# Unchosen spans of the picked sums: overwritten on VectorE instead of by a TensorE product, and a seventh picked slot

## The reference

```python
edge_index = jnp.stack([src, dst])
h = jnp.maximum(_layernorm(x, axis=-1), 0.0)
x = x + _L0_gnn_ref(h, edge_index, edge_attr_32, ...)     # relu([h[dst], h[src], attr] @ W1 + b1) @ W2 + b2, segment_sum
h = jnp.maximum(_layernorm(x, axis=-1), 0.0)
x = x + _L1_gnn_ref(h, edge_weight1, src, dst)            # softmax(edge weight) per dst times h[src], segment_sum, elu
h = jnp.maximum(_layernorm(x, axis=-1), 0.0)
x = x + _L2_gnn_ref(h, theta_w, theta_b, phi_w, phi_b, src, dst)  # (h[dst] - h[src]) @ theta + phi(h[src]), segment_max
h = jnp.maximum(_layernorm(x, axis=-1), 0.0)
x = x + _L3_gnn_ref(h, edge_index, edge_attr_16, ...)     # three-layer MLP on [h[src], h[dst], attr], segment mean
```

## Time and profile before

| | |
|---|---|
| median of 3 runs | 7793.15 us (7792.11 to 7808.14) |
| the profiled execution | 7796.36 us, of which the span of instructions is 7794.6 us |
| granted TensorE clock, mean | 0.941 |
| PE (matmul) busy | 6659.6 us, 85% |
| DVE busy | 5210.7 us, 67% |
| POOL busy | 5823.6 us, 75% |
| ACT busy | 2085.6 us, 27% |

### The profile page before, as it was taken

The page is one execution under the profiler, slowest core; times in us unless marked ns, Lnnn a source line. Parts: engine busy times, 40 slices in busy tenths (PEclk is TensorE's granted clock), DMA queues, the critical chain, the costliest instruction groups (busy, mean ns, idle before and its releaser), DMA issues.

```text
span 7794.6 us, 87563 instructions
## 1 busy us (share of the span) xinstructions
PE 6659.6 (85%) x29454; PEld 5473.0 (70%) x29454; DVE 5210.7 (67%) x6271; ACT 2085.6 (27%) x5004; POOL 5823.6 (75%) x6117
## 2 busy tenths in 40 slices
PE   0799999999669999999479999999139999999992
PEld 0688888888557777777367777777127777777771
DVE  6577777777667777777767777777545666666663
ACT  5133333333212222222300000000014444444441
POOL 7777777777777777777767777777777777777776
PEclk9999999999879999999689999999569999999995
DMA  8354544444323333333223333333124444444441
GB/s 321 84 113 112 113 111 113 112 112 113 84 62 83 82 82 88 82 82 82 59 63 74 74 74 77 75 74 74 44 59 98 100 98 98 98 98 99 98 99 42
DMA packets 1063994, 722.05 MB, mean 93 GB/s; under 512 B 583026, under 2 KB 970916, under 8 KB 1063428
## 3 DMA queue, kind: packets, MB, share of 16 engines
q1 hardware_dynamic: 850448, 510.81, 23.7%
q0 software_dynamic: 197008, 163.26, 13.7%
q10 hardware_dynamic: 16100, 42.39, 1.4%
HBM read 478.38 MB, written 237.49 MB: 92 GB/s over the span
## 4 chain that ended last, share of the span: by engine, by line
POOL 48%; issue 16%; PE 6%; DVE 3%; DMA 1%; ACT 0%; POOLq 0%; DVEq 0%
POOL G L683 42%; POOL R L702 5%; PE pOdd L905 4%; PE pRows L905 1%; POOL first_rows L644 1%; DVE onehot L1288 1%; DVE S L1337 1%; PE pRows L1002 0%; PE pOdd L897 0%; DVE G L1300 0%; ACT G L828 0%; DMA G<-table,e_dst 0%; DMA G<-table,idx 0%; DVE pT L1322 0%; DMA prefix<-O 0%
## 5 line engine op out<-in xcount | busy, mean ns | idle before, releaser
L683 POOL DMA_INDIRECT G<-table,idx x2923 | 2758.3, 944 | 891.0 <-issue 878.2
L683 POOL DMA_INDIRECT G<-table,e_dst x2497 | 2362.8, 946 | 790.7 <-issue 753.7
L1223 DVE TENSOR_TENSOR_SCAN K<-mask_f,K,pT 48x512 f32<-48x512 bf16 x782 | 1005.4, 1286 | 1242.5 <-PE pT L970 1117.0
L1002 PEld LDWEIGHTS pRows<-w,S 128*128 128x128 f32 x6256 | 1573.9, 324 | 304.4 <-issue 179.2
L905 PE MATMUL pOdd<-h_high,onehot 128*128 128x480 f32 (+1 forms) x3880 | 1519.5, 392 | 0.0
L905 PE MATMUL pOdd<-h_low,onehot 128*128 128x480 f32 (+1 forms) x3880 | 1489.6, 384 | 0.0
L1002 PE MATMUL pRows<-w,S 128*128 128x48 f32 x6256 | 1445.3, 374 | 2.1 <-ACT O L838 0.5
L905 PE MATMUL pRows<-h_high,onehot 128*128 128x480 f32 (+1 forms) x2430 | 952.6, 392 | 85.1 <-DVE h_low L1076 85.1
L905 PE MATMUL pRows<-h_low,onehot 128*128 128x480 f32 (+1 forms) x2430 | 920.4, 379 | 0.0
L1288 DVE TENSOR_TENSOR onehot<-mask_f,pEven 128x2560 fp32r<-128x2560 f32 (+1 forms) x390 | 892.1, 2288 | 19.4 <-DMA mask_f<-pick_row 19.4
L905 PEld LDWEIGHTS pOdd<-h_high,onehot 128*128 128x128 f32 x3880 | 749.8, 193 | 128.5 <-issue 3.9
(11 more groups left out here) (203 smaller groups left out, 8666.6 us busy)
## 6 DMA issues: line engine op xcount, KB each, us to landing
mask_f<-same_row SPq DMA_DIRECT2D x392, 256.0 KB, 3.3
prefix<-O SPq DMA_DIRECT2D x194, 512.0 KB, 3.6
G<-first_rows SPq DMA_DIRECT2D x784, 96.0 KB
prefix<-O SPq DMA_DIRECT2D x390, 192.0 KB
G<-table,idx POOLq DMA_INDIRECT x2923
G<-table,e_dst POOLq DMA_INDIRECT x2497
first_rows<-zeros ACTq DMA_DIRECT2D x14, 2688.0 KB, 15.5
K<-in_ea_dram SPq DMA_DIRECT2D x588, 64.0 KB
```

Of the source, the lines that this page charges most:

```text
L683: pool.indirect_dma_start(rows[:, slot, j, 0:widths[l]], None, table[l], bass.IndirectOffsetOnAxis(ap=at[:, n, j:j + 1], axis=0))\
L1002: last = pe.matmul(o, s[:, :, j], (w2_0 if l == 0 else w3_3)[:, :], start=True, stop=True)
L1223: dve.tensor_tensor_scan(K[r, c.slot, :], mask_of(c, r), pT[c.slot % 2][r, :], K[r, (c.slot - 1) % RING, CHUNK - 1:CHUNK], ALU.mult, ALU.add)\
```

## The change

The hiding product and `minus_big` go. The accumulation now starts with the first group's product. Ahead of each reduction VectorE runs one `scalar_tensor_tensor` in place on the accumulator, sums = unchosen * -3e38 + sums, over all picks of the duo, and waits for its completion (`link`). The same operation is placed in `place_edges` for layers 0 and 3. Slot 4 joins `PICK_SLOTS`, so seven of eight chunks pick in layers 1 and 2; `PICK_EXTRA` goes. In layers 0 and 3 the picked columns stay the same.

```diff
@@ -45,8 +45,7 @@
 QUAD = 32
 QUADS = P // QUAD
 PICK_SPAN = 10
-PICK_SLOTS = (1, 2, 3, 5, 6, 7)
-PICK_EXTRA = RING + 4
+PICK_SLOTS = (1, 2, 3, 4, 5, 6, 7)
 PICK_COLUMN = TJ - 1
 PICK_RING = 4
 EDGE_PICK_CYCLE = {0: 3, 3: 6}
...
@@ -59,7 +58,7 @@
 
 def stream_picks(chunks):
 
-    return [n for n in range(chunks) if n % RING in PICK_SLOTS or n % (2 * RING) == PICK_EXTRA]
+    return [n for n in range(chunks) if n % RING in PICK_SLOTS]
 
 
 def edge_picks(l, chunks):
...
@@ -892,25 +890,14 @@
                                              start=True, stop=True)
                         last.then_inc(hq_made, 1)
 
-            def hide_unchosen(out, i):
-
-                pe.matmul(out[:, 0:SPAN * D], minus_big[:, :],
-                          unchosen[:, i, :].rearrange("p (s o) -> p s o", o=1).to_broadcast([P, SPAN, D]),
-                          start=True, stop=False)
-
             def add_group(out, rows_of, g):
 
                 first, stop = g * SPAN, min((g + 1) * SPAN, B)
                 for part in (h_high, h_low):
                     last = pe.matmul(out[:, 0:(stop - first) * D], rows_of[:, g, :],
                                      part[:, first:stop, :].rearrange("p b d -> p (b d)"),
-                                     start=False, stop=g == PICK_GROUPS - 1 and part is h_low)
+                                     start=g == 0 and part is h_high, stop=g == PICK_GROUPS - 1 and part is h_low)
                 return last
-
-            def hide_unchosen_of(d):
-
-                for k, i in enumerate(picks_of(d)):
-                    hide_unchosen(pick_sum[d % 2][:, k, :], i)
 
             def add_rows(d, g):
 
...
@@ -935,7 +920,6 @@
                     pe.wait_ge(split_made, SPLIT_BEFORE[l] + 1)
                 for d in range(first, DUOS):
                     pe.wait_ge(picks_marked[l], d + 1 - FIRST_DUO[l])
-                    hide_unchosen_of(d)
                     for g in range(PICK_GROUPS):
                         last = add_rows(d, g)
                     last.then_inc(picks_summed[l], 1)
...
@@ -1014,7 +997,6 @@
                         if k == 0:
                             pe.wait_ge(edges_marked, EDGE_PICKS_BEFORE[l] + i + 1)
                             pe.wait_ge(split_made, SPLIT_BEFORE[l] + (1 if l == 0 else NQ))
-                            hide_unchosen(out, FIRST_PICK[l] + i)
                         for g in range(PICK_GROUPS * k // steps, PICK_GROUPS * (k + 1) // steps):
                             last = add_group(out, edge_onehot[i % len(edge_sum[l])], g)
                         if k == steps - 1:
...
@@ -1230,11 +1211,14 @@
                     if i is None:
                         return
                     dve.wait_ge(edges_summed, EDGE_PICKS_BEFORE[l] + i + 1)
-                    place_edges(i, c.slot, PICK_COLUMN)
-
-                def place_edges(i, slot, j, l=l):
+                    place_edges(i, FIRST_PICK[l] + i, c.slot, PICK_COLUMN)
+
+                def place_edges(i, flags, slot, j, l=l):
 
                     out = edge_sum[l][i % len(edge_sum[l])]
+                    sums = out[:, 0:SPAN * D].rearrange("p (b d) -> p b d", d=D)
+                    link(dve.scalar_tensor_tensor(sums, unchosen[:, flags, :].rearrange("p (b o) -> p b o", o=1)
+                                                  .to_broadcast([P, SPAN, D]), -BIG, sums, ALU.mult, ALU.add))
                     dve.tensor_reduce(G[:, slot, j, 0:D],
                                       out[:, 0:SPAN * D].rearrange("p (b d) -> p d b", d=D), AX, ALU.max)
 
...
@@ -1290,6 +1274,13 @@
                                       span_id.rearrange("p (k g o) -> p k g o", k=1, o=1)
                                       .to_broadcast([P, k, PICK_GROUPS, P]), ALU.is_equal).then_inc(picks_marked[l], 1)
 
+                def hide_unchosen(sums, i, k):
+
+                    sums = sums.rearrange("p k (b d) -> p k b d", d=D)
+                    flags = unchosen[:, i:i + k, :].rearrange("p k (b o) -> p k b o", o=1)
+                    link(dve.scalar_tensor_tensor(sums, flags.to_broadcast([P, k, SPAN, D]), -BIG, sums,
+                                                  ALU.mult, ALU.add))
+
                 def place_picks(d, l=l):
 
                     if d >= DUOS:
...
@@ -1297,6 +1288,7 @@
                     dve.wait_ge(picks_summed[l], d + 1 - FIRST_DUO[l])
                     picks = picks_of(d)
                     k, slot = len(picks), PICKS[picks[0]] % RING
+                    hide_unchosen(pick_sum[d % 2][:, 0:k, 0:SPAN * D], picks[0], k)
                     last = dve.tensor_reduce(G4[:, slot:slot + k, PICK_COLUMN, 0:D],
                                              pick_sum[d % 2][:, 0:k, 0:SPAN * D]
                                              .rearrange("p k (b d) -> p k d b", d=D), AX, ALU.max)
```

More of the change, by code:

```diff
@@ L189, in build @@
         ident = sb("ident", [P, P])
-        minus_big = sb("minus_big", [P, P], bf16)
         w1_0 = sb("w1_0", [P, HID])
@@ L863, in _ @@
         def _(pe):
-            pe.wait_ge(ident_done, 2)
+            pe.wait_ge(ident_done, 1)
             pe.wait_ge(G_zeroed, 1)
@@ L928, in sum_picks @@
                         for d in range(2):
-                            if g == 0:
-                                hide_unchosen_of(d)
                             last = add_rows(d, g)
@@ L954, in _ @@
                         out = edge_sum[0][i % 2]
-                        hide_unchosen(out, NP + i)
                         for g in range(PICK_GROUPS):
@@ L1147, in _ @@
             dve.wait_ge(ident_done, 1)
-            dve.tensor_scalar(minus_big[:, :], ident[:, :], -BIG, None, ALU.mult).then_inc(ident_done, 1)
             link(dve.tensor_tensor(seed[:, 0:1], ident[:, 49:50], ident[:, 82:83], ALU.add))
@@ L1368, in _ @@
                             n, j = EARLY[i - 2]
-                            place_edges(i, n % RING, j)
+                            place_edges(i, NP + i - 2, n % RING, j)
                         if i < len(EARLY):
```

## The result

| | before | after |
|---|---|---|
| median of the runs, us | 7792.63 | 8042.57 |
| its range, us | 7791.38 to 7808.14 | 8039.82 to 8046.96 |
| span of the profiled execution, us | 7794.6 | 8044.3 |
| mean granted clock of TensorE | 0.941 | 0.922 |

The change makes the kernel slower: the ratio is 1.0317, interval 1.0299 to 1.0334. The direction and the mechanism in layers 1 and 2 were forecast; the size and a loss in layer 3 were not, and 8042.6 lies above the range.

What follows compares the result with a forecast made beforehand. The prediction took GpSimd's gathers as the bound before, the TensorE - VectorE loop after: 7796.4 + 44 (loop and edges) + 73 (clock falls) = 7913 us for the profiled execution, so 7910 for the median; range 7835 to 8000.

Steps and rivals of the forecast that it cites:

- What bounds the kernel, and that the bound moves: Layers 1 and 2: GpSimd's gathers set the pace before; afterwards the TensorE - VectorE loop, 32.4 us a turn against 31.2.
- Part 3: VectorE's new operation in layers 1 and 2 stands inside the loop: 1.16 us for 960 elements, 1.20 us with its completion.
- far bound (0.6, 2.2): Limits for the new operation's time: 0.6 us if elements overlapped, 2.2 us if the accumulator were passed once each way.
- The loop without the clock: Layers 1 and 2 with TensorE's clock staying up: turns of 32.4 us, +44 us in total, 7840 us.
- The 0.12 us added to s1: Added per turn in layers 1 and 2, for a 128x128 float32 weight load now first after TensorE's wait.
- Part 4: TensorE's clock in layers 1 and 2: about 2.2 us idle every turn can bring falls costing 1.55 us each; +73 us.
- I take half the turns: Layers 1 and 2: clock falls assumed in half the turns, giving +73 us.
- the case "every turn": Layers 1 and 2: a clock fall in every turn, 94 x 1.55 = 146 us, time near 7983 us.
- Rival (a): Layers 1 and 2: the loop bounds but TensorE's clock stays up, 7837 us; chance 0.20.
- Layers 0 and 3 "come out at nothing": No cost in layers 0 and 3: VectorE's added 0.7 us in three or six chunks lies under its waits for TensorE.
- The bound named there, 99 us: Most that layers 0 and 3 would cost if VectorE's waits gave no cover: 142 x 0.7 = 99 us.
- Parts 1 and 2: Layers 1 and 2: 50 fewer gathers, worth 62.4 us if GpSimd stays the bound; TensorE's work 29.9 us under GpSimd's 31.2.

Runs made afterwards that it cites:

- the filler kernel: Changed kernel plus five TensorE products that nobody reads after each one-pick sum in layers 1 and 2: 7912.68 us, ratio 1.0133 to the kernel before.
- The one-product filler: Changed kernel plus one unread TensorE product, instead of five, after each one-pick sum in layers 1 and 2: 7997.08 us, ratio 1.0248.
- the last experiment: Kernel before the change with slot 4 always picked and layers 1 and 2's scans behind the one-hot, no VectorE operation: 7759.32 us, ratio 0.9935.

## Why the prediction was right in kind and wrong in size

**What bounds the kernel, and that the bound moves: right.** GpSimd's waits for VectorE's scan are there (145.8 us in layer 1; the forecast of some 60 was for the loop without falls, and the filler kernel, which has none, shows 75.6), and s1 starts on the one-hot.

**Part 3, the operation: right.** 1.163 us for 960 elements, 1.20 with the step to the reduction; forecast 1.16 and 1.20. The neighbouring rows of the same operation and the same memory gave it, and neither far bound (0.6, 2.2) had anything in it.

**The loop without the clock: right.** A turn of 32.44 us against 32.4; +25.1 and +25.8 us in the layers, by the filler kernel, against +21 and +23. The last 7 us are the allowance of 2 us a layer for the edges and 0.03 to 0.04 us a turn. The 0.12 us added to s1 had no row behind it; s1 without a fall takes 8.67 us, s2 and s3 8.57, so about that much is there. That the weight load is the reason, no run shows.

**Part 4, the clock: the mechanism right, the term mis-sized.** The idle was forecast at about 2.2 us and is 2.16; a fall at 1.55 us and is 1.53. What failed is "I take half the turns". Falls came in 43 of 48 turns in each layer, 131.5 us instead of 73. The rows before gave 2.08 (never) and 2.24 to 2.44 (five of six), and I read a threshold out of them, with 2.2 "between". The one-product filler shows that there is no sharp edge: 1.94 us in every turn, less than the 2.08 that brought no fall in the kernel before, did so in half the turns. That waits of this size were rare there, and return in every turn now, is the likely reason that their rate did not carry over; this is argued, no run tests it. The prediction had the case "every turn" worked out at 146 us and near 7983. Rival (a) falls: 86 falls stand behind 2.16 us of idle. The Trainium skill allows idle gaps of that length ("TensorE: Matmul & The Clock Gate", Why this matters for your kernels); this trace disagrees with it, and the measurement decides.

**Layers 0 and 3 "come out at nothing": wrong, and it put the time out of the range.** Layer 3 cost 60.7 us. The step that failed is "0.7 us more on VectorE in three or six chunks lies under its waits for TensorE". It set a total of waits against a total of added work. VectorE does wait in most chunks, but in the one chunk of six where the place, the one-hot and the scan meet, it is the other way round: TensorE, which has no time to spare in this layer, waits for the scan, 62 times and 40.2 us in all. It also left out that a fall of the clock can follow so short a wait. The bound named there, 99 us "that cover gone", would have held it, but the range left it out: with 7983 for falls in every turn and 60 us more, the forecast's own numbers reach 8043. The falls carry the loss: 46 of them at 1.6 us are 74 us, more than the 60.7 measured over the layer; where the rest is won back was not followed up. Why 46 of 62 equal waits bring a fall and 16 do not stays open. For layer 0 "nothing" was right. From 500 to 2050 us TensorE waits for the scan there once, for 0.5 us, and the 5.6 us by which layer 1 starts later are no sign of the operation: layer 1 starts at 2219.9 us with it in the run with the scan behind the one-hot, as in the kernel before, and at 2227.1 in the last experiment, where the product hides the spans in every layer.

**Parts 1 and 2: right, but as read there.** "Read alone, this says that the change wins" held once the loop was cut: with the scan behind the one-hot, GpSimd's back-to-back gathers end at 3744.4 with the new operation in place, against 3775.7 before: 31.3 us for 25 gathers, where the prediction has 31.2.

Summed over the stages: 51 us loop, 131.5 us falls, 60.7 us layer 3, 6.6 us the start and the rest, 250 in all.

## What to carry to other kernels

When work is added to an engine that waits half its time, look for the step with the most queued ahead of what another engine needs next, in every phase of the kernel; totals and means over chunks hide it. Before such an operation is given up, see whether something stands between it and the consumer that the consumer doesn't need: here a scan moved by one place in the order of VectorE's stages (behind the one-hot in layers 1 and 2, ahead of it in layer 3) turned 3.2% slower into 0.7% faster. And where an added wait leaves TensorE idle by two microseconds in every turn, count the half-rate stretch behind it in every turn, and try filler or reordering before trusting an average.

## What the runs showed of the hardware that was not expected

- In these runs the clock of TensorE has no single length of idle at which it falls. In layers 1 and 2, idle of 0.74 to 1.08 us in each turn brought no fall, 1.94 us falls in about half the turns and in runs, 2.16 us in 43 of 48 with the exceptions at nearly regular distance, 3.35 us in all.
- In layer 3 a wait of only 0.65 us, among short products and transposes, is followed by a fall 46 times of 62, 1.6 to 3.0 us after it ends, and all of these falls go when the wait goes.
- A product whose result nobody reads can pay: five of them per turn took 131.5 us off layers 1 and 2.
- Scalar-tensor-tensor in place on the accumulator, with a broadcast fp8 operand, takes 1.163 us for 960 elements and 0.631 us for 480: no more than a reduction over the same elements (1.157 and 0.657 us).
